# Vision mamba block with attention: scores over 64 rows, step sizes over 128 rows, and a scratch computation ahead of the loop

## The chip, the core and the metric

The kernel runs on one core of a Trainium2 chip. The metric is the device time of one execution in microseconds (us). The kernel before took 6128.99 us, the median of three runs (6116.84, 6128.99 and 6130.85). All data are float32.

## The reference, cut to what matters

For each of 32 images (the first 16 are "large", the others "small") the reference builds 274 tokens of 192 channels, passes them through a bidirectional selective scan, and then through a block with attention and an MLP:

```python
# per image: x is (274, 192)
h = concat([cls, patches @ W + b]) + pos_emb, then concat text      # 1 + 196 + 77 = 274 tokens
# mixer, for the forward and the backward direction
dt_lo, B, C = split(conv_silu(xi) @ x_proj)                         # dt_lo has 12 values per token
dt = softplus(dt_lo @ dt_w + dt_b)                                  # 384 step sizes per token
state = exp(dt * A) * state + (dt * u) * B;  y = state . C          # 16 states per channel
# attention, 12 heads of 16 values
a = softmax((q @ k.T) * 16 ** -0.5);  o = a @ v;  x = x + o @ w_proj + b_proj
# small images: the gated sum of three variants of the attention and of the MLP
x = x + gelu(ln(x) @ w1 + b1) @ w2 + b2
```

## The kernel before, in words

One step of the program handles one image (b) and interleaves three stages that belong to different images: the scans of image b in both directions, the fine part (layer norms, attention, MLP) of the image before it (f, ending with e), and the front part (patch projection, input projection, convolution, step sizes) of the image after it (a). A step is cut into 2 x 18 "gaps". Each engine has its own instruction stream, written out by hand: in every gap it issues its share of the scan, then its share of the fine part, then its share of the front. Two loops (7 iterations for large and 6 for small images, two steps in each) hold 26 of the 32 steps, the other six are written out; before them stands `front()`, after them `finish()`, in which only the last fine part is left and nothing overlaps it. Order is kept by semaphores alone: each engine works its list strictly in order and stops at a wait.

- VectorE (DVE) carries the scan (`scan_step`): in a cycle of three gaps it multiplies (L936, 128x2192), scans (L953) and multiplies again (L957). L936 may start only when TensorE has summed the states of two half-units before (`ysum`, L417). DVE also takes the row maxima of the scores (L1062), the reciprocal of the row sums (L1069) and the products with it (L1072).
- ScalarE (ACT) computes the decays (L715), the exponentials of the softmax (L788) and most copies out of PSUM; `qk_copy` (L773) copies queries and keys of a group of four heads from PSUM to `qk`, scaling the queries by -1/4.
- TensorE (PE) sums the 8 state rows with an identity matrix (L417) and does all projections. `scores` (L530) multiplies, for each of 12 heads and 3 tiles of 92 queries, 16 rows of queries by 16 rows of keys: head hd of a group lies in the rows 32 * (hd % 4) to 32 * (hd % 4) + 16, and the 16 rows behind it are zero, since the projection weights are spaced with zeros. `turn` (L542) transposes the probabilities, `av` (L551) multiplies them by the values. `dt_mm` (L479) computes the step sizes over 13 rows: 12 of `dt_lo` and one of ones for the bias. Every float32 matmul appears in the trace as two matmul records.
- Each of `qk_mms`, `qk_copy` and `scores` is done per group: group 0 in gaps 11 to 13, group 1 in gaps 17 to 18, group 2 in gaps 22 to 23. In PE's list the scores of a head wait for the copies of the group, and from the second head on for the exponentials of the head before.
- In `front()`, SyncE (SP) loads the patches, the text and 14 weights; DVE fills constants, waits for all weights (semaphore s_w), derives some constants from them and raises s_c to 20; PE and ACT wait for that before the first image. GpSimd (POOL) only makes the identity matrix and a mask.

## Time and profile before

| | |
|---|---|
| median of three runs | 6128.99 us (6116.84 to 6130.85) |
| span of the profiled execution | 6123.8 us; the page gives no time of that execution beside its span; the median is 5.2 us above the span |
| busy: DVE, PE, ACT, POOL | 5554.8, 5309.5, 3780.6, 0.8 us |
| mean granted TensorE clock | 0.874 of full speed |
| weights landed, first instruction that needed them | 25.72 us |

The span is the time from the first to the last instruction. Busy shares are means over the whole span. In rows of the trace, "PEclk" is the granted clock of TensorE: 1.00 is 2.4 GHz, 0.50 is 1.2 GHz, and values between are a mix of the two over the stretch. "idle before <-releaser" is how long the engine had done nothing, and what ended that.

### The profile page before, as it was taken

Reading aid. Unit: us, or ns where it says so; the run is one execution under the profiler, and the core shown is the slowest. Engines: PE = TensorE matmul, PEld = TensorE weight load, DVE = VectorE, ACT = ScalarE, POOL = GpSimd, SP = SyncE. Lnnn points to the kernel's source line nnn. Section 1 sums busy time; section 2 is a strip of 40 time slices with the busy share of each in tenths; the row PEclk is TensorE's granted clock in tenths of the full one; section 3 lists DMA queues with packets and bytes.
Section 4 is the critical chain, followed back from the end, with each engine's and each line's share of the span. In section 5 each row is a group of like instructions: output and inputs, shape, how many; then the busy total and the mean of one; then the engine's idle time right before and its main releaser. Section 6 shows DMA issues by size and latency. Waiting matters only on the chain.

```text
span 6123.8 us, 74116 instructions
## 1 busy us (share of the span) xinstructions
PE 5309.5 (87%) x22816; PEld 3509.9 (57%) x22816; DVE 5554.8 (91%) x6069; ACT 3780.6 (62%) x9506; POOL 0.8 (0%) x8
## 2 busy tenths in 40 slices
PE   5788888888888888888889999888998989989888
PEld 3555555555555555555556655655656556556554
DVE  6999999999999999999999999998999989999962
ACT  3566666656666556666666666666666666666643
POOL 0000000000000000000000000000000000000000
PEclk7898888888888888888989988898888888889885
DMA  3211211211211211211221111111111212112100
GB/s 101 64 45 57 64 45 53 66 51 51 64 52 46 66 58 44 65 53 44 65 65 42 60 60 38 64 58 44 64 45 54 66 37 65 50 47 65 40 23 2
DMA packets 56934, 327.85 MB, mean 54 GB/s; under 512 B 13246, under 2 KB 15742, under 8 KB 23627
## 3 DMA queue, kind: packets, MB, share of 16 engines
q1 hardware_dynamic: 56490, 322.53, 16.6%
q8 instruction: 207, 3.39, 0.2%
q14 instruction: 237, 1.93, 0.1%
HBM read 313.52 MB, written 8.98 MB: 53 GB/s over the span
## 4 chain that ended last, share of the span: by engine, by line
PE 40%; DVE 33%; issue 20%; ACT 6%; DVEq 1%; DMA 0%; SPq 0%; ACTq 0%
DVE hs L953 12%; PE y_ps L417 10%; PE f_ps L530 7%; DVE hs L936 4%; PE f_ps L542 4%; DVE hs L957 4%; PE f_ps L581 3%; PE f_ps L496 2%; PE a_ps L455 2%; DVE neg_max L1062 2%; DVE xc L1016 2%; PE f_ps L511 2%; PE f_ps L592 2%; PE f_ps L487 2%; PE a_ps L465 1%
## 5 line engine op out<-in xcount | busy, mean ns | idle before, releaser
L953 DVE TENSOR_TENSOR_SCAN hs<-decay,hs 128x2192 f32<-128x2192 f32 x384 | 1811.1, 4717 | 28.0 <-issue 19.7
L417 PE MATMUL y_ps<-hs,ident 128*128 128x274 f32 x5376 | 1719.8, 455 | 89.5 <-issue 31.3
L715 ACT ACTIVATE decay<-dt,inner_s 128x273 f32<-128x273 f32 x3072 | 1380.6, 513 | 75.7 <-issue 40.3
L417 PEld LDWEIGHTS y_ps<-hs,ident 128*128 128x128 f32 x5376 | 1104.1, 217 | 480.8 <-issue 187.8
L936 DVE TENSOR_TENSOR hs<-b_rows,dtu 128x2192 f32<-128x2192 f32 x384 | 935.5, 2436 | 99.2 <-PE y_ps L417 76.7
L957 DVE TENSOR_TENSOR hs<-hs,c_rows 128x2192 f32<-128x2192 f32 x384 | 934.7, 2434 | 3.4
L530 PE MATMUL f_ps<-qk 16*92 16x274 f32 x2304 | 733.5, 458 | 227.9 <-ACT hid L788 216.4
L805 ACT ACTIVATE hid<-f_ps 92x273 f32<-92x273 f32 (+1 forms) x1152 | 421.7, 393 | 556.6 <-PE f_ps L542 552.4
L788 ACT ACTIVATE hid<-f_ps,neg_max 92x274 f32<-92x274 f32 x1152 | 544.0, 480 | 301.1 <-DVE neg_max L1062 300.9
L530 PEld LDWEIGHTS f_ps<-qk 16*92 16x92 f32 x2304 | 350.7, 174 | 549.2 <-ACT hid L788 344.6
L542 PE MATMUL f_ps<-ident,hid 92*92 92x92 f32 x3456 | 514.7, 286 | 86.8 <-ACT hid L805 48.7
L542 PEld LDWEIGHTS f_ps<-ident,hid 92*92 92x92 f32 x3456 | 386.0, 148 | 341.6 <-issue 162.1
L1062 DVE TENSOR_REDUCE neg_max<-f_ps 92x1 f32<-92x274 f32 x1152 | 446.8, 430 | 72.0 <-PE f_ps L530 69.4
L455 PE MATMUL a_ps<-xn,w_in_s 96*128 96x274 f32 x1536 | 464.7, 428 | 8.5 <-ACT xi L738 4.9
L496 PE MATMUL f_ps<-res,centre_w 96*96 96x274 f32 x768 | 238.0, 460 | 202.6 <-DVE res L1040 128.6
L722 ACT ACTIVATE hid<-f_ps 96x548 f32<-96x548 f32 x128 | 79.2, 619 | 465.5 <-PE f_ps L496 465.5
L455 PEld LDWEIGHTS a_ps<-xn,w_in_s 96*128 96x128 f32 x1536 | 304.8, 209 | 90.9 <-issue 15.5
L592 PE MATMUL f_ps<-hid,fc_s 128*96 128x274 f32 x1152 | 294.5, 409 | 53.2 <-ACT hid L826 51.3
L1016 DVE SCALAR_TENSOR_TENSOR xc<-xi,inner_s,xc 128x274 f32<-128x274 f32 x576 | 289.6, 504 | 20.1
L496 PEld LDWEIGHTS f_ps<-res,centre_w 96*96 96x96 f32 x768 | 134.4, 186 | 296.0 <-DVE res L1040 142.4
L592 PEld LDWEIGHTS f_ps<-hid,fc_s 128*96 128x96 f32 x1152 | 192.7, 169 | 145.7 <-ACT hid L826 63.7
L819 ACT ACTIVATE hid<-f_ps,fc_b_s 128x274 f32<-128x274 f32 x384 | 183.1, 490 | 136.7 <-PE f_ps L581 136.7
(103 smaller groups left out, 5773.8 us busy)
## 6 DMA issues: line engine op xcount, KB each, us to landing
b_rows<-bc_rows SPq DMA_DIRECT2D x128, 1096.0 KB, 5.6
c_rows<-bc_rows SPq DMA_DIRECT2D x128, 1096.0 KB, 5.6
xp<-in_patches SPq DMA_DIRECT2D x32, 588.0 KB, 7.4
out<-h SPq DMA_DIRECT2D x32, 205.5 KB, 2.2
bc_rows<-bc_s SPq DMA_DIRECT2D x64, 34.2 KB, 1.5
h<-in_txt SPq DMA_DIRECT2D x32, 57.8 KB, 2.3
w_in_s<-in_w_in SPq DMA_DIRECT2D x1, 1152.0 KB
fc_s<-in_fc SPq DMA_DIRECT2D x2, 576.0 KB
```

The lines of the kernel that those rows point to most:

```text
L417: mm = pe.matmul(y_ps[:, 0:T], ident[:, :], hs[q % 2][:, n, :], start=(q % 2 == 0 and n == 0), stop=(q % 2 == 1 and n == end - 1))
L455: mm = pe.matmul(a_ps[:, j % 2, 0:T], w_in_s[:, i, d, j * 128:(j + 1) * 128], xn[parity(b)][:, i, :], start=(i == 0), stop=(i == 1))
L496: mm = pe.matmul(f_ps[0:CH, o, 0:T], centre_w[:, int(i != o), :], x[:, i, :], start=(i == 0), stop=(i == 1))
L530: pe.matmul(f_ps[0:QT, t, 0:T], qk[r:r + HD, 0, QS[t]:QS[t] + QT], qk[r:r + HD, 1, :], start=True, stop=True).then_inc(sc_mm, 1)
L542: mm = pe.transpose(f_ps[0:QT, 3 + n % 2, k * QT:(k + 1) * QT], prob[hd % 2][:, t, QS[k]:QS[k] + QT], ident[0:QT, 0:QT])
L592: mm = pe.matmul(f_ps[0:CH, VARIANTS[v][2][i], 0:T], fc2_s[:, ch, i * CH:(i + 1) * CH], hid[:, HC * v + ch, :], start=(ch == 0), stop=(ch ...
L715: e = act.activation(decay[half][:, n, t], dt[d][:, u, t], ACT.Exp, scale=inner_s[:, d, u, s:s + 1])
L788: act.activation(prob[hd % 2][:, t, :], f_ps[0:QT, t, 0:T], ACT.Exp, scale=-1.0, bias=neg_max[:, hd % 2, t:t + 1], accum_out=row_sum[:, hd ...
L936: dve.tensor_tensor(x[:, :, :], states[half][:, :, :], dtu[d][:, u, :].unsqueeze(1).broadcast_to([128, NH, T]), ALU.mult).then_inc(dbu_don ...
L953: dve.tensor_tensor_scan(i, a, i, 0.0, ALU.mult, ALU.add).then_inc(scan_done, 1)
L957: dve.tensor_tensor(x[:, :, :], x[:, :, :], reads[half][:, :, :], ALU.mult)\
L1062: dve.tensor_reduce(neg_max[:, hd % 2, t:t + 1], f_ps[0:QT, t, 0:T], AX_X, ALU.min)\
```

## The change

Three things, in one diff.

1. Scores contract over 64 rows. ACT now makes two copies of the queries of a group, each multiplied by a column of `q_scale` that is -1/4 in the rows of the even (or the odd) heads and 0 elsewhere, and one of the keys: three copies in place of two. A score matmul takes 64 rows (two heads); the rows of the other head are zero in the masked copy.
2. Step sizes contract over 128 rows. `dt_w_s` and `dt_lo` are widened to 128 rows; POOL zeroes all of `dt_w_s` before SP loads its 13 rows, and SP waits for that before the first weight.
3. A scratch computation in the prologue, whose results nothing uses: 17 counted instructions on DVE, 9 products on POOL, 20 matmuls on PE over 32 or 64 rows (40 records in a trace), and 2 exponentials on ACT. DVE reaches the wait for the weights only when all four are done. ACT's table load moves ahead of it.

```diff
--- before.py
+++ after.py
@@ -126,7 +126,7 @@
         w_in_s = sb("w_in_s", [CH, 2, 2, 2 * INNER])
         inner_s = sb("inner_s", [128, 2, IC, INNER_W])
         x_proj_s = sb("x_proj_s", [128, 2, IC, 32 + 2 * N])
-        dt_w_s = sb("dt_w_s", [RANK + 1, 2, INNER])
+        dt_w_s = sb("dt_w_s", [128, 2, INNER])
         w_out_s = sb("w_out_s", [128, 2, IC, C])
         w_qk_s = sb("w_qk_s", [CH, 2, 2, GROUPS * 128])
         w_v_s = sb("w_v_s", [CH, 2, C + HD])
@@ -141,6 +141,7 @@
         mean_w = sb("mean_w", [CH, CH])
         centre_w = sb("centre_w", [CH, 2, CH])
         v_mask = sb("v_mask", [QT, 3])
+        q_scale = sb("q_scale", [128, 2])
         eps_c = sb("eps_c", [128, 1])
         one_c = sb("one_c", [128, 1])
 
@@ -159,13 +160,13 @@
         dt = [sb(f"dt{d}", [128, IC, T]) for d in range(2)]
         dtu = [sb(f"dtu{d}", [128, IC, T]) for d in range(2)]
         bc_s = sb("bc_s", [32 + 2 * N, T])
-        dt_lo = sb("dt_lo", [RANK + 1, T])
+        dt_lo = sb("dt_lo", [128, T])
         states = [sb(f"b_rows{i}", [128, NH, T]) for i in range(2)]
         reads = [sb(f"c_rows{i}", [128, NH, T]) for i in range(2)]
         decay = [sb(f"decay{i}", [128, NH, T]) for i in range(2)]
         hs = [sb(f"hs{i}", [128, NH, T]) for i in range(2)]
         yg = sb("yg", [128, UNITS, T])
-        qk = sb("qk", [128, 2, T])
+        qk = sb("qk", [128, 3, T])
         v_s = sb("v_s", [QT, 3, C + HD])
 
         hid = sb("hid", [128, 3 * HC, T])
@@ -190,6 +191,10 @@
         s_cp = sem("constants_pool")
         s_ca = sem("constants_act")
         s_x = sem("patches_loaded")
+        p_dve = sem("probe_vector")
+        p_pool = sem("probe_pool")
+        p_pe = sem("probe_tensor")
+        p_act = sem("probe_scalar")
         s_txt = [sem(f"txt_loaded{i}") for i in range(2)]
 
         tok_mm = sem("tok_mm")
@@ -267,7 +272,7 @@
         out_stored = sem("out_stored")
 
         LOADS = [(tok_w_s, tok_w), (feat_s, feat), (w_in_s, w_in), (inner_s, inner), (x_proj_s, x_proj),
-                 (dt_w_s, dt_w), (w_out_s, w_out), (w_qk_s, w_qk), (w_v_s, w_v), (w_proj_s, w_proj),
+                 (dt_w_s[0:RANK + 1, :, :], dt_w), (w_out_s, w_out), (w_qk_s, w_qk), (w_v_s, w_v), (w_proj_s, w_proj),
                  (fc1_s, fc1), (fc1_b_s, fc1_b), (fc2_s, fc2), (gate, gumbel)]
         CONSTS = 20
 
@@ -364,6 +369,7 @@
             def front():
                 load_patches((0, 0))
                 load_txt((0, 0))
+                sp.wait_ge(s_cp, 1)
                 for dst, src in LOADS:
                     sp.dma_start(dst[tuple(slice(None) for _ in dst.shape)], src).then_inc(s_w, 16)
                 spread_rows((0, 0), 0)
@@ -389,13 +395,23 @@
 
         @block.gpsimd
         def _(pool):
+            pool.memset(dt_w_s[:, :, :], 0.0).then_inc(s_cp, 1)
             pool.memset(ident[:, :], 0.0).then_inc(s_cp, 1)
             pool.memset(v_mask[:, :], 1.0).then_inc(s_cp, 1)
-            pool.wait_ge(s_cp, 2)
+            pool.wait_ge(s_cp, 3)
             pool.affine_select(out=ident[:, :], in_=ident[:, :], compare_op=ALU.not_equal, fill=1.0, base=0,
                                pattern=[[-1, 128]], channel_multiplier=1).then_inc(s_cp, 1)
 
             pool.memset(v_mask[0:1, 1:3], 0.0).then_inc(s_cp, 1)
+            pool.memset(q_scale[:, :], 0.0).then_inc(s_cp, 1)
+            pool.wait_ge(s_cp, 6)
+            for r in range(4):
+                pool.memset(q_scale[32 * r:32 * r + 32, r % 2:r % 2 + 1], -HD ** -0.5).then_inc(s_cp, 1)
+            pool.wait_ge(s_cp, 10)
+            pool.wait_ge(p_dve, 7)
+            for n in range(9):
+                wait(pool, p_pool, n)
+                pool.tensor_tensor(hs[1][:, 4:8, :], hid[:, 0:4, :], hid[:, 4:8, :], ALU.mult).then_inc(p_pool, 1)
 
 
         @block.tensor
@@ -520,14 +536,14 @@
                     mm.then_inc(v_mm, 1)
 
             def scores(f, hd):
-                g, r = hd // 4, 32 * (hd % 4)
-                pe.wait_ge(qk_copied, at(f, 2 * GROUPS, 2 * g + 2))
+                g, rows = hd // 4, slice(64 * (hd % 4 // 2), 64 * (hd % 4 // 2) + 64)
+                pe.wait_ge(qk_copied, at(f, 3 * GROUPS, 3 * g + 3))
                 if hd == 0:
                     pe.wait_ge(v_copied, at(f, 3, 3))
                 for t in range(3):
                     if hd > 0:
                         pe.wait_ge(pexp, at(f, 3 * HEADS, 3 * hd - 2 + t))
-                    pe.matmul(f_ps[0:QT, t, 0:T], qk[r:r + HD, 0, QS[t]:QS[t] + QT], qk[r:r + HD, 1, :],
+                    pe.matmul(f_ps[0:QT, t, 0:T], qk[rows, hd % 2, QS[t]:QS[t] + QT], qk[rows, 2, :],
                               start=True, stop=True).then_inc(sc_mm, 1)
 
             def turn(f, hd, lo, hi):
@@ -674,9 +690,27 @@
                             out_proj(b, (UNITS - 2,))
                         fronts(b, d, a, gap)
 
+            def scratch():
+                pe.wait_ge(s_cp, 10)
+                pe.wait_ge(p_dve, 17)
+                for _ in range(2):
+                    for r in range(4):
+                        rows = slice(32 * r, 32 * r + 32)
+                        mm = pe.matmul(f_ps[0:QT, r, 0:T], ident[rows, 0:QT], hid[rows, 0, :], start=True, stop=True)
+                for _ in range(3):
+                    for r in range(2):
+                        rows = slice(32 * r, 32 * r + 32)
+                        mm = pe.matmul(f_ps[0:QT, r, 0:T], ident[rows, 0:QT], hid[rows, 0, :], start=True, stop=True)
+                for _ in range(3):
+                    for r in range(2):
+                        rows = slice(64 * r, 64 * r + 64)
+                        mm = pe.matmul(f_ps[0:QT, r, 0:T], ident[rows, 0:QT], hid[rows, 0, :], start=True, stop=True)
+                mm.then_inc(p_pe, 1)
+
             def front():
+                scratch()
                 pe.wait_ge(s_w, 16 * len(LOADS))
-                pe.wait_ge(s_cp, 4)
+                pe.wait_ge(s_cp, 10)
                 pe.wait_ge(s_c, CONSTS)
                 b = (0, 0)
                 tok(b, (0, 1))
@@ -765,13 +799,13 @@
                 act.activation(v, v, ACT.Ln, bias=one_c[:, 0:1]).then_inc(sp_ln, 1)
 
             def qk_copy(f, g):
-                for s in range(2):
-                    act.wait_ge(qk_mm, at(f, 2 * GROUPS, 2 * g + s + 1))
-                    if s == 0:
-                        wait(act, sc_mm, at(f, 3 * HEADS, 12 * g))
-
-                    act.activation(qk[:, s, :], f_ps[:, s, 0:T], ACT.Copy, scale=(-HD ** -0.5, 1.0)[s])\
+                act.wait_ge(qk_mm, at(f, 2 * GROUPS, 2 * g + 1))
+                wait(act, sc_mm, at(f, 3 * HEADS, 12 * g))
+                for odd in range(2):
+                    act.activation(qk[:, odd, :], f_ps[:, 0, 0:T], ACT.Copy, scale=q_scale[:, odd:odd + 1])\
                         .then_inc(qk_copied, 1)
+                act.wait_ge(qk_mm, at(f, 2 * GROUPS, 2 * g + 2))
+                act.activation(qk[:, 2, :], f_ps[:, 1, 0:T], ACT.Copy).then_inc(qk_copied, 1)
 
             def v_copy(f):
                 for t in range(3):
@@ -893,10 +927,13 @@
                             fine_late(*part)
 
             def front():
+                act.preload_act_table_set("natural_log_exp_and_others")
+                act.wait_ge(p_pe, 1)
+                act.activation(hid[0:QT, 9:11, :], f_ps[0:QT, 0:2, 0:T], ACT.Exp, scale=-1.0).then_inc(p_act, 1)
+                act.activation(hid[0:QT, 11:13, :], f_ps[0:QT, 0:2, 0:T], ACT.Exp, scale=-1.0).then_inc(p_act, 1)
                 act.wait_ge(s_w, 16 * len(LOADS))
-                act.wait_ge(s_cp, 4)
+                act.wait_ge(s_cp, 10)
                 act.wait_ge(s_c, CONSTS)
-                act.preload_act_table_set("natural_log_exp_and_others")
                 act.activation(inner_s[:, :, :, I_A:I_A + N], inner_s[:, :, :, I_A:I_A + N], ACT.Exp).then_inc(s_ca, 1)
                 b = (0, 0)
                 squares(xn[0][:, :, :], sq_a, a_cen, 1, a_sq)
@@ -1178,6 +1215,52 @@
                             fine(*part)
                         fronts(b, d, a, gap)
 
+            def scratch():
+                u = f_ps[:, 0:3, :].rearrange("p b t -> p (b t)")
+                u_in = u[:, 0:4 * T]
+                u_row = u[:, 4 * T:5 * T]
+                a = hid[:, 0:4, :].rearrange("p n t -> p (n t)")
+                o = hs[1][:, 0:4, :].rearrange("p n t -> p (n t)")
+                dec = decay[1][:, 0:4, :].rearrange("p n t -> p (n t)")
+                dve.memset(hid[:, :, :], 0.5).then_inc(p_dve, 1)
+                dve.memset(decay[1][:, :, :], 0.5).then_inc(p_dve, 1)
+                dve.wait_ge(p_dve, 2)
+                dve.tensor_tensor(u_in, a, dec, ALU.mult).then_inc(p_dve, 1)
+                dve.wait_ge(p_dve, 3)
+                dve.tensor_tensor_scan(o, dec, u_in, 0.0, ALU.mult, ALU.add).then_inc(p_dve, 1)
+                dve.wait_ge(p_dve, 4)
+                dve.tensor_scalar(u_row, hid[:, 0, :], 0.5, None, ALU.mult).then_inc(p_dve, 1)
+                dve.wait_ge(p_dve, 5)
+                dve.tensor_tensor(u_in.rearrange("p (n t) -> p n t", n=4), hid[:, 0:4, :],
+                                  u_row.unsqueeze(1).broadcast_to([128, 4, T]), ALU.mult).then_inc(p_dve, 1)
+                dve.wait_ge(p_dve, 6)
+                dve.tensor_tensor_scan(o, dec, u_in, 0.0, ALU.mult, ALU.add).then_inc(p_dve, 1)
+                dve.wait_ge(p_pool, 1)
+                dve.wait_ge(p_dve, 7)
+                dve.tensor_tensor_scan(o, dec, u_in, 0.0, ALU.mult, ALU.add).then_inc(p_dve, 1)
+                dve.wait_ge(p_dve, 8)
+                dve.tensor_tensor(u_in.rearrange("p (n t) -> p n t", n=4), hid[:, 0:4, :],
+                                  u_row.unsqueeze(1).broadcast_to([128, 4, T]), ALU.mult).then_inc(p_dve, 1)
+                dve.wait_ge(p_dve, 9)
+                dve.tensor_tensor_scan(o, dec, u_in, 0.0, ALU.mult, ALU.add).then_inc(p_dve, 1)
+                dve.wait_ge(p_dve, 10)
+                dve.scalar_tensor_tensor(out=decay[1][:, 4, :], in0=u_row, scalar=0.5, in1=hid[:, 9, :],
+                                         op0=ALU.mult, op1=ALU.add).then_inc(p_dve, 1)
+                dve.tensor_reduce(neg_max[:, 0, 0:2], f_ps[0:QT, 0:2, 0:T], AX_X, ALU.min).then_inc(p_dve, 1)
+                dve.wait_ge(p_dve, 12)
+                dve.tensor_scalar(u_row, hid[:, 0, :], 0.5, None, ALU.mult).then_inc(p_dve, 1)
+                dve.wait_ge(p_dve, 13)
+                dve.tensor_tensor(u_row, hid[:, 0, :], hid[:, 1, :], ALU.mult).then_inc(p_dve, 1)
+                dve.wait_ge(p_dve, 14)
+                dve.tensor_tensor(decay[1][:, 5, :], hid[:, 0, :], hid[:, 1, :], ALU.mult).then_inc(p_dve, 1)
+                dve.wait_ge(p_dve, 15)
+                dve.tensor_tensor(u_in, a, dec, ALU.mult).then_inc(p_dve, 1)
+                dve.wait_ge(p_dve, 16)
+                dve.tensor_tensor_scan(o, dec, u_in, 0.0, ALU.mult, ALU.add).then_inc(p_dve, 1)
+                dve.wait_ge(p_pool, 9)
+                dve.wait_ge(p_dve, 17)
+                dve.wait_ge(p_act, 2)
+
             def front():
 
                 dve.memset(mean_w[:, :], 1.0 / C).then_inc(s_c, 1)
@@ -1185,6 +1268,7 @@
                 dve.memset(one_c[:, :], 1.0).then_inc(s_c, 1)
                 dve.memset(xi[:, :, :], 0.0).then_inc(s_c, 1)
                 dve.memset(dt_lo[:, :], 1.0).then_inc(s_c, 1)
+                scratch()
                 dve.wait_ge(s_w, 16 * len(LOADS))
                 for i in range(2):
 
@@ -1199,7 +1283,7 @@
                 dve.tensor_reduce(gate_sum[:, 0:1], gate[:, 0:3], AX_X, ALU.add).then_inc(s_c, 1)
                 dve.tensor_copy(gate_sum[:, 1:2], gate[:, 0:1]).then_inc(s_c, 1)
                 dve.wait_ge(s_c, 14)
-                dve.wait_ge(s_cp, 4)
+                dve.wait_ge(s_cp, 10)
                 dve.tensor_tensor(centre_w[:, 0, :], ident[0:CH, 0:CH], mean_w[:, :], ALU.subtract).then_inc(s_c, 1)
                 dve.tensor_scalar(centre_w[:, 1, :], mean_w[:, :], -1.0, None, ALU.mult).then_inc(s_c, 1)
                 for i in range(2):
```

## Rows read from the trace of the kernel before

**Rows 1.** The page: busy us (share) and instructions of each engine.

```profile
PE 5309.5 (87%) x22816; PEld 3509.9 (57%) x22816; DVE 5554.8 (91%) x6069; ACT 3780.6 (62%) x9506; POOL 0.8 (0%) x8
```

**Rows 2.** DVE's waits, whole span: us in total, times, longest us.

```profile
DVE hs L936 <- PE y_ps L417: 76.7, 77, 1.9
DVE neg_max L1062 <- PE f_ps L530: 69.4, 76, 8.0
DVE row_inv L1069 <- ACT hid L788: 27.3, 19, 2.5
```

**Rows 3.** DVE's waits in the last attention, 5985 to 6075 us; same columns.

```profile
DVE neg_max L1062 <- PE f_ps L530: 47.8, 29, 8.0
DVE row_inv L1069 <- ACT hid L788: 7.5, 3, 2.5
```

**Rows 4.** Windows: length, busy us (count) of PE, PEld, DVE, ACT, POOL, PEclk, DMA.

```profile
2085.00:2090.00 5.00, 5.00 (x24) 3.75 (x23) 4.26 (x4) 3.50 (x8) 0.00 (x0) 1.00 0.00 0
2105.00:2110.00 5.00, 5.00 (x16) 3.25 (x15) 4.96 (x9) 1.68 (x5) 0.00 (x0) 0.50 0.71 226
2097.00:2174.00 77.00, 68.75 (x318) 43.55 (x319) 75.48 (x112) 55.77 (x169) 0.00 (x0) 0.83 0.14 45
2174.00:2277.00 103.00, 88.11 (x376) 61.25 (x374) 96.58 (x76) 57.61 (x123) 0.00 (x0) 0.95 0.20 64
5985.00:6070.00 85.00, 72.69 (x283) 40.51 (x282) 24.57 (x72) 39.58 (x129) 0.00 (x0) 0.56 0.00 1
```

**Rows 5.** Timeline: start, us, engine, line, count; two waits, and scores at 0.50.

```profile
2088.45 2.44 DVE L936 TENSOR_TENSOR hs<-b_rows,dtu 128x2192 f32<-128x2192 f32 x1 [0.74 <-PE y_ps L417]
2361.89 2.44 DVE L936 TENSOR_TENSOR hs<-b_rows,dtu 128x2192 f32<-128x2192 f32 x1 [1.91 <-PE y_ps L417]
6040.23 3.01 PE L530 MATMUL f_ps<-qk 16*92 16x274 f32 x6 [1.04 <-ACT hid L788]
```

**Rows 6.** Timeline around the copies of group 1, step at 2071 us.

```profile
2119.94 2.43 DVE L936 TENSOR_TENSOR hs<-b_rows,dtu 128x2192 f32<-128x2192 f32 x1
2120.50 0.92 ACT L773 ACTIVATE qk<-f_ps 128x274 f32<-128x274 f32 x2
2121.55 1.61 PE L530 MATMUL f_ps<-qk 16*92 16x274 f32 x6 [0.33 <-ACT qk L773]
2122.73 0.90 DVE L1062 TENSOR_REDUCE neg_max<-f_ps 92x1 f32<-92x274 f32 x2
```

**Rows 7.** Timeline around the copies of group 2, same step.

```profile
2146.11 1.62 PE L530 MATMUL f_ps<-qk 16*92 16x274 f32 x6
2149.87 1.13 DVE L1062 TENSOR_REDUCE neg_max<-f_ps 92x1 f32<-92x274 f32 x3
```

**Rows 8.** Groups by line and shape: busy us, mean ns | idle before.

```profile
L953 DVE TENSOR_TENSOR_SCAN hs<-decay,hs 128x2192 f32<-128x2192 f32 x384 | 1811.1, 4717 | 28.0 <-issue 19.7 <-DVE decay L943 1.5
L961 DVE TENSOR_TENSOR hs<-hs 128x1096 f32<-128x1096 f32 x96 | 124.8, 1300 | 3.3
L773 ACT ACTIVATE qk<-f_ps 128x274 f32<-128x274 f32 x192 | 76.7, 400 | 90.7 <-PE f_ps L511 84.1
L417 PE MATMUL y_ps<-hs,ident 128*128 128x274 f32 x5376 | 1719.8, 455 | 89.5 <-issue 31.3 <-DVE hs L961 29.8 <-DVE yg L970 20.9
L479 PE MATMUL a_ps<-dt_lo,dt_w_s 13*128 13x274 f32 x384 | 140.8, 447 | 6.6 <-DVE dt L1022 5.9 <-ACT dt_lo L750 0.5
```

**Rows 9.** Timeline of the prologue.

```profile
1.12 0.76 DVE L1186 MEMSET xi<- 128x840 f32 x1
1.22 0.29 POOL L395 TENSOR_SCALAR_AFFINE_SELECT ident<-ident 128x128 f32<-128x128 f32 x1 [0.23 <-POOL v_mask L393]
1.97 0.58 SPq L368 DMA_DIRECT2D tok_w_s<-in_tok_w  x1
25.72 0.23 DVE L1192 TENSOR_TENSOR h<-feat_s 96x1 f32<-96x1 f32 x2 [23.56 <-DMA gate<-in_gumbel]
27.86 5.88 PE L429 MATMUL a_ps<-xp,tok_w_s 128*96 128x196 f32 x24 [27.86 <-DVE bias_sum L1207]
```

## Prediction

> **What bounds the kernel now.** I read the page's busy times first, then DVE's waits, the clock in windows, and the timeline. DVE is busy 5554.8 of 6123.8 us [rows 1], so 569 us of the span are time in which DVE idles, and the change touches no DVE instruction of the loop: the loop can only gain from that idle time. Much of it lies outside the loop's steps (in the prologue and in the last image's fine part, which nothing overlaps), or waits for things that the change doesn't touch, such as the layer norms' rstd. Three waits can hang on the scores' stretch. The row maxima wait for score matmuls: 69.4 us, of which 47.8 are in the last attention, so 21.6 in the steps [rows 2, 3]. The reciprocal waits for the exponentials: 27.3 less 7.5, 19.8 us. L936 waits for the state sums: 76.7 us in 77 waits, but most of these come once or twice per image at full clock as a fixed 0.74 us (one is shown; I count about 48 of 0.74 to 0.77), some 36 us; the rest, about 41 us, sits 14 to 20 us behind the last scores of an image and reaches 1.91 us each [rows 2, 5]. Together 82 us.
>
> That these waits are tied to the clock is what the windows show. From 2174 to 2277 us, mostly outside the attention, the granted clock is 0.95; from 2097 to 2174, the attention of the same image, it is 0.83 [rows 4]. In the attention PE is no idler: from 2105 to 2110 it is busy all 5 us and yet granted 0.50, while from 2085 to 2090 it is as busy at 1.00. What differs is what it does: before 2105 it does scores over 16 rows and transposes, before 2085 state sums over 128 rows. In the last attention (5985 to 6070) it is busy 72.69 of 85 us at 0.56 [rows 4]. I read this as a clock that falls where matmuls use few rows, though busy. The change makes the same matmuls use 64.
>
> **The change part by part.**
>
> *Score matmuls.* 2304 records stay 2304; six take 1.61 us at 1.00 and 3.01 at 0.50 [rows 5, 6]. More rows need no more time at a given clock: the 13-row step sizes take 447 ns on average, about the 455 ns of the 128-row state sums [rows 8]. I take 0 directly. The gain is the clock. Upper bound: all 82 us. Lower bound: nothing. The attention's dips to 0.50 come in two kinds: where PE is busy with few rows, and where it idles, waiting for DVE or ACT. Four times the rows in the scores should remove the first kind and leave the second. I take half, 41 us, and expect the clock of such an attention to go from 0.83 to about 0.90, and the mean of the span from 0.874 to about 0.90.
>
> *Last attention.* DVE, ACT and PE follow one another here, so time at 0.50 counts in full: 12 heads x (3.01 - 1.61) = 16.8 us for the scores alone. But PE idles between heads and the transposes keep their rows, so I expect the clock to stay mostly low and take a quarter, 4 us (0 to 17).
>
> *Step sizes over 128 rows.* 384 records, same columns: 0. They lie outside the low stretches, so no clock is bought either. The wider `dt_lo` memset has the same 274 columns.
>
> *Third copy.* 96 more copies of 0.40 us [rows 8], 38 us on ACT, which is 62% busy. The scores of a group wait for all copies, so for group 1 the first score starts 0.40 us later. Timeline: DVE's L936 ends at 2119.94 + 2.43 = 2122.37, the scores run from 2121.55 to 2123.16, and the maxima end at 2122.73 + 0.90 = 2123.63, right behind the scores; 0.40 us later the last maximum ends about 0.3 us later [rows 6]. 31 x 0.3 = 9 us. For group 2 scores begin at 2146.11 and the maxima only at 2149.87, since DVE is in its product [rows 7]: hidden, and if that cover went it would be 12 us. Group 0 lies a gap and more ahead of its scores. Behind the copy in ACT's list stand three decays of the next scan, with slack. In the last attention 3 x 0.40 = 1 us. Sum 10 us, between 0 and 38.
>
> *SP's wait for the zeroed weights.* SP's first weight goes out at 1.97; POOL starts a memset of 768 columns at about 0.75 and needs 1 to 2 us by its 0.29 us for 128 columns [rows 9]. At most 0.6 us, on loads that no longer set the end, below.
>
> *Scratch.* Before, DVE passes the wait for the weights at 25.72 [rows 9]. Now it gets there when the scratch is done. DVE starts it at about 2.2. Memsets of 4932 and 2192 columns at 0.76 us for 840: 6.4. Four products of 1096 columns at 1.30: 5.2. Five scans of 1096 columns at half of 4.717: 11.8. Six small ones, the maximum over 548 columns counted twice, 7 x 0.45: 3.1 [rows 6, 8, 9]. Before the third scan DVE waits for POOL's first product. No row has one; DVE's 1.30 is the floor, POOL's select (0.29 for 128 columns, so 2.5 for 1096) the nearest row and the ceiling; I take 2.5. DVE is done at 31.2. POOL's nine products start at 16.4 and end at 38.9, under what follows. Then PE's 40 records: 0.27 each at full clock is 10.8 us; at 0.50 all the way 20; and 4.3 if matmuls of different row groups overlap (16 in place of 40). I take 10.8, end 42.0. Then two exponentials over 548 columns, 0.8 each by the copies: 43.6. The wait for weights is long over, so the prologue is longer by 43.6 - 25.7 = 17.9. One credit: PE's first 24 projection records, 5.88 us now, would take 24 x 0.27 x 196/274 = 4.6 if the scratch has raised the clock. Net +17 us, between 9 (POOL at 1.3, PE at 4.3) and 27 (PE at 20, no credit). The earlier table load gives nothing: it stood beside PE's first projections.
>
> The Trainium skill (TensorE: Matmul & The Clock Gate, Part 3: Packing small matmuls) says that matmuls in distinct row groups run concurrently; no row here shows it. By it the scratch would take PE 4.3 us and the total would be 6 us lower.
>
> *Sum.* -41 - 4 + 10 + 17 = -18. The page gives the span, 6123.8, and not the time of its execution; the span lies 5.2 us under the median, within the spread of the three runs, and the differences apply to both: 6129 - 18 = 6111 us, a span of 6106.
>
> **The rivals.**
>
> *The clock doesn't care about rows (slower).* If the dips come from something else that scores and transposes share (their short bursts, the waits between heads), 64 rows buy nothing and only the costs stay: 6129 + 10 + 17 = 6156, 6138 to 6194 with their bounds. For it speaks that the dips also come where PE waits; against it, the 5 us at 0.50 with PE busy all through [rows 4]. It decides from the point where the clock gives back less than 27 us. The Trainium skill's page TensorE: Matmul & The Clock Gate (Part 1, What's actually happening) says that the gate follows how busy PE has been, with no word of rows; its Part 4 says that transposes don't count as busy in the same way. By that rule the scores already count in full and this rival is what happens, at 6156; the busy 5 us at 0.50 speak against its first half, and partly for its second.
>
> *The clock rises, DVE does not profit.* The attention's clock goes up, but PE's work arrives in time anyway: DVE is busy 75.48 of 77 us there [rows 4]. Waits for state sums stay, as the dip behind the last scores comes from PE idling. Then the gain is some 10 us: 6129 - 10 + 27 = 6146. For it: 1.5 us of idle time in a whole attention. Against: the 1.91 and the reciprocal's waits.
>
> *The clock stays up through every attention.* All 82 us and the tail's 17 go: 6129 - 82 - 17 + 27 = 6057. Against: dips where PE has nothing to do, which no row count cures.
>
> **How the numbers follow.** My forecast has a chance of 0.45, with its own range 6090 to 6132; the clock without regard to rows 0.17; no profit 0.22; full clock 0.16. A measurement here tells 0.3% from no change, 18 us: below 6110.6 is faster, above 6147.4 slower. The forecast stands on that bound and gives 0.27 to faster and 0.18 to same; the full clock 0.16 to faster; no profit 0.19 to same and 0.03 to slower; the first rival 0.06 to same and 0.11 to slower. Faster 0.43, same 0.43, slower 0.14. The range takes in most of the outer cases: 6070 to 6155. I name 6111.
>
> **What would show it.** In the profile after: mean clock near 0.90, and above 0.87 in an attention of the middle of the run (else the first rival). The reciprocal's waits and the row maxima's outside the last attention should halve (else no profit). The six score records of a head still take 1.61 us at full clock. Copies x288 at 0.40. The first projection at about 45 rather than 27.9; its start is the price of the scratch, and if it is near 35 matmuls overlapped. The prediction fails if the low stretches merely move to the projections behind the attention, or if ACT's third copy holds up scores of every group.

## The result, and the profile after

The changed kernel took 6066.69 us (median of four runs, 6062.72 to 6075.44), 0.990 of the time of before (0.988 to 0.992). I had predicted 6111 and a range of 6070 to 6155: the direction was right and the size was not.

The page of the changed kernel: span, then busy us (share) and instructions of each engine.

```profile
span 6065.1 us, 74390 instructions
PE 5150.6 (85%) x22856; PEld 3475.0 (57%) x22856; DVE 5575.6 (92%) x6086; ACT 3813.9 (63%) x9604; POOL 25.4 (0%) x23
```

DVE is busy 20.8 us longer than in [rows 1], the scratch, and yet the span is 58.7 us shorter. So DVE idled about 80 us less. Where it stopped idling, DVE's waits over the whole span of the changed kernel (us in total, times, longest us):

```profile
DVE neg_max L1099 <- PE f_ps L546: 50.1, 32, 8.2
DVE hs L973 <- PE y_ps L433: 38.6, 64, 1.2
DVE row_inv L1106 <- ACT hid L822: 10.9, 9, 2.5
```

They answer to [rows 2], with the lines moved by the edit: L936 is L973, L1062 is L1099, L1069 is L1106. The wait for state sums is half of what it was, and its longest fell from 1.9 to 1.2 us. Of the row maxima's 50.1 us, 49.7 are in the last attention (5920 to 6016 us), where [rows 3] had 47.8: in the steps that wait is gone, and in the last attention it has not shrunk.

Windows of the changed kernel, to set beside [rows 4]: the attention of a large image, the stretch behind it, the attention of a small image, and the last attention (length, busy us (count) of PE, PEld, DVE, ACT, POOL, PEclk, DMA share, GB/s).

```profile
2106.00:2183.00 77.00, 67.81 (x319) 42.19 (x320) 75.98 (x111) 57.60 (x172) 0.00 (x0) 0.83 0.14 44
2183.00:2286.00 103.00, 85.48 (x378) 61.67 (x376) 96.72 (x81) 58.79 (x128) 0.00 (x0) 0.96 0.21 64
4104.00:4181.00 77.00, 66.00 (x320) 41.50 (x321) 75.96 (x112) 57.18 (x172) 0.00 (x0) 0.87 0.14 45
5928.00:6008.00 80.00, 69.29 (x267) 38.33 (x265) 24.58 (x72) 39.39 (x128) 0.00 (x0) 0.53 0.00 1
```

The same window over a small image in the kernel before:

```profile
4112.00:4189.00 77.00, 69.88 (x313) 44.61 (x314) 74.22 (x111) 54.42 (x164) 0.00 (x0) 0.78 0.14 45
```

The small image's clock rose from 0.78 to 0.87. The large image's window shows 0.83 again: a mean over one hand-cut window depends on where it is cut and on the image. So I took the same stretch in every image, from the start of its first score to the start of its last one. The mean granted clock there is 0.863 before and 0.894 after for large images, 0.813 and 0.899 for small ones, and 0.558 and 0.534 in the last attention, whose stretch takes 68.0 and 69.6 us. Behind the scores, up to the first score of the next image, it stayed where it was (0.898 and 0.894 for large images, 0.929 and 0.928 for small ones), so the low stretches did not move there. The mean clock of the whole span is 0.894 (0.874 before).

### The profile page after: what moved, and what is told of

Its sections match the earlier page's. It is cut to its first block, busy times and chain, and to the rows that moved or that the text cites. A ratio compares the mean times of both kernels' runs of the same rounds, so it can differ in the third digit from the quotient of the medians.

```text
span 6065.1 us, 74390 instructions
## 1 busy us (share of the span) xinstructions
PE 5150.6 (85%) x22856; PEld 3475.0 (57%) x22856; DVE 5575.6 (92%) x6086; ACT 3813.9 (63%) x9604; POOL 25.4 (0%) x23
## 4 chain that ended last, share of the span: by engine, by line
DVE 41%; PE 28%; issue 23%; ACT 6%; DVEq 1%; ACTq 0%; DMA 0%; POOL 0%; POOLq 0%
DVE hs L990 14%; PE y_ps L433 6%; DVE hs L973 5%; DVE hs L994 4%; DVE neg_max L1099 4%; PE f_ps L546 4%; PE f_ps L597 3%; DVE xc L1053 3%; PE f_ps L608 3%; PE f_ps L512 3%; PE f_ps L503 2%; PE f_ps L558 2%; DVE hid L1109 2%; ACT hid L822 2%; PE a_ps L471 1%
## 5 line engine op out<-in xcount | busy, mean ns | idle before, releaser
L433 PE MATMUL y_ps<-hs,ident 128*128 128x274 f32 x5376 | 1643.9, 440 | 80.2 <-DVE hs L998 29.8
L433 PEld LDWEIGHTS y_ps<-hs,ident 128*128 128x128 f32 x5376 | 1091.8, 212 | 407.7 <-issue 113.7
L973 DVE TENSOR_TENSOR hs<-b_rows,dtu 128x2192 f32<-128x2192 f32 x384 | 935.3, 2436 | 63.1 <-PE y_ps L433 38.6
L546 PE MATMUL f_ps<-qk 64*92 64x274 f32 x2304 | 712.0, 448 | 294.2 <-ACT hid L822 275.7
L546 PEld LDWEIGHTS f_ps<-qk 64*92 64x92 f32 x2304 | 339.7, 172 | 609.9 <-ACT hid L822 414.4
L558 PE MATMUL f_ps<-ident,hid 92*92 92x92 f32 x3456 | 479.5, 272 | 106.5 <-DVE hid L1109 68.7
L558 PEld LDWEIGHTS f_ps<-ident,hid 92*92 92x92 f32 x3456 | 357.1, 139 | 343.6 <-issue 143.0
L1099 DVE TENSOR_REDUCE neg_max<-f_ps 92x1 f32<-92x274 f32 x1152 | 437.7, 428 | 51.8 <-PE f_ps L546 50.1
## 6 DMA issues: line engine op xcount, KB each, us to landing
bc_rows<-bc_s SPq DMA_DIRECT2D x64, 34.2 KB, 1.5
```

Source lines behind the costliest of these rows:

```text
L433: mm = pe.matmul(y_ps[:, 0:T], ident[:, :], hs[q % 2][:, n, :], start=(q % 2 == 0 and n == 0), stop=(q % 2 == 1 and n == end - 1))
L546: pe.matmul(f_ps[0:QT, t, 0:T], qk[rows, hd % 2, QS[t]:QS[t] + QT], qk[rows, 2, :], start=True, stop=True).then_inc(sc_mm, 1)
L558: mm = pe.transpose(f_ps[0:QT, 3 + n % 2, k * QT:(k + 1) * QT], prob[hd % 2][:, t, QS[k]:QS[k] + QT], ident[0:QT, 0:QT])
L973: dve.tensor_tensor(x[:, :, :], states[half][:, :, :], dtu[d][:, u, :].unsqueeze(1).broadcast_to([128, NH, T]), ALU.mult).then_inc(dbu_don ...
L1099: dve.tensor_reduce(neg_max[:, hd % 2, t:t + 1], f_ps[0:QT, t, 0:T], AX_X, ALU.min)\
```

## The experiments

All kernels in one table. Ratios are to the kernel before, with the 95% interval. The columns prologue, loop and tail split the profiled span into the prologue (up to the first patch addition), the loop, and the tail (from the last image's patch addition). "Three waits" are DVE's for state sums, row maxima and reciprocals, between the prologue and the last fine part.

| kernel | median us | ratio (interval) | mean clock | prologue | loop | tail | three waits |
|---|---|---|---|---|---|---|---|
| before | 6129.9 | 1 | .874 | 33.9 | 5566.8 | 523.2 | 118.0 |
| after | 6066.7 | .990 (.988, .992) | .894 | 57.0 | 5495.4 | 512.7 | 42.4 |
| e1 no scratch | 6058.4 | .989 (.987, .991) | .895 | 34.7 | 5509.1 | 512.8 | 38.9 |
| e2 scores alone | 6071.4 | .991 (.990, .993) | .899 | 34.4 | 5524.6 | 518.5 | 82.3 |
| e3 copies, 16 rows | 6146.8 | 1.004 (1.002, 1.005) | .872 | 33.3 | 5580.3 | 530.3 | 127.3 |
| e4 scratch alone | 6121.9 | 1.000 (.999, 1.001) | .877 | 57.1 | 5529.9 | 530.8 | |
| e5 e1 + 20 fills | 6048.7 | .986 (.984, .988) | .892 | 34.6 | 5499.1 | 512.6 | |
| e6 32 rows, 2 copies | 6074.5 | .990 (.988, .992) | .887 | 33.4 | 5520.0 | 516.6 | 81.7 |
| e7 128 rows, 5 copies | 6047.4 | .986 (.984, .988) | .929 | 34.8 | 5517.6 | 489.2 | 78.7 |
| e8 step sizes alone | 6134.3 | 1.000 (.999, 1.001) | .866 | 35.2 | 5588.3 | 525.6 | 95.4 |
| e9 before + 20 fills | 6115.2 | .997 (.996, .999) | .871 | 34.2 | 5569.9 | 527.5 | |
| e10 no POOL products | 6060.9 | .988 (.986, .990) | .892 | 47.8 | 5499.5 | 512.7 | |
| e11 e2 + 20 fills | 6060.1 | .989 (.986, .991) | .902 | 34.5 | 5505.9 | 516.0 | |
| e12 best version | 6030.6 | .983 (.982, .985) | .896 | 33.6 | 5503.1 | 492.1 | |

The median of before is the one measured beside the changed kernel; beside e1 to e4 it was 6126.3, beside e5 to e8 6131.6, beside the others 6131.0. A profile is of one execution: those of e2, e8 and e9 were 8, 17 and 18 us longer than their kernels' medians, so their splits are read with care.

The experiments keep small parts of the changed kernel's prologue: all but e9 zero `dt_w_s` on POOL ahead of the weights' loads, fill `q_scale`, and load ACT's table early, also where the steps don't need it. Without the scratch their prologues lie within 1.3 us of before's 33.9, so "alone" below is meant for the steps.

### Rows or copies: e1, e2, e3, e6, e7

**e1** is the change without its third part.

```diff
-                scratch()          # PE and DVE
-            for n in range(9):     # POOL's products
-                act.activation(hid[0:QT, 9:11, :], ...)   # and the second exponential
```

> The change without the scratch computation (scores over 64 rows, three copies, step sizes over 128 rows). If the scratch costs only what it adds ahead of the first projection (23.2 us from the first tile's addition in the two traces, 33.85 against 57.02), this takes 23 us less than the changed kernel: about 6044 us, ratio 0.986 to before, with the clock of the changed kernel, 0.89. Rival: the scratch shifts the loop against the clock's own rhythm or leaves the clock high, and part of the gain in the loop is its doing; then this is no faster than the changed kernel, 6060 or more.

It came 8 us under the changed kernel, but the intervals overlap: the whole gain is there without the scratch. Of the two expectations the second came true: no 23 us are saved with it.

**e2** also takes the step sizes back to 13 rows.

```diff
-        dt_w_s = sb("dt_w_s", [128, ...])
-        dt_lo = sb("dt_lo", [128, T])
+        dt_w_s = sb("dt_w_s", [RANK + 1, ...])
+        dt_lo = sb("dt_lo", [RANK + 1, T])
```

> Only the scores are changed (64 rows, three copies); the step sizes stay at 13 rows, no scratch. If the step sizes do nothing, this equals the kernel without the scratch within 0.2%, about 6044 us. Rival: the 128 rows of the step sizes hold the clock up in the gaps before the next scores (or at the loop's turn), and without them 10 to 30 us come back.

**e3** keeps e2's three copies, the masks included, and lets the scores contract over 16 rows as before. It differs from e2 in nothing but the rows that each score matmul reads.

```diff
-                g, rows = hd // 4, slice(64 * (hd % 4 // 2), 64 * (hd % 4 // 2) + 64)
+                g, rows = hd // 4, slice(32 * (hd % 4), 32 * (hd % 4) + HD)
```

> The same three copies and masked queries, but each score matmul takes 16 rows again; all else as in the kernel with the scores alone changed. Work, waits and order are the same; only the rows differ. If the rows raise the clock, the mean clock falls back to 0.87 and the time goes to before plus the third copy: 6130 to 6140 us. Rival: the gain comes from the third copy's delay shifting the steps, not from rows; then this keeps the gain and takes 6044 to 6060.

This is the pair that decides: 6146.8 against 6071.4 us, with intervals far apart. The same instructions, the same columns, and 64 rows in place of 16 are worth 75 us. It took a little more than the 6130 to 6140 I had expected of it. DVE's waits outside the prologue and the last fine part show how. Those of e3:

```profile
DVE hs L947 <- PE y_ps L428: 76.2, 76, 1.9
DVE row_inv L1080 <- ACT hid L799: 25.7, 22, 1.3
DVE neg_max L1073 <- PE f_ps L541: 25.4, 51, 3.8
DVE yg L981 <- PE y_ps L428: 23.8, 13, 3.7
```

And those of e2, same columns:

```profile
DVE hs L947 <- PE y_ps L428: 66.3, 76, 1.9
DVE yg L981 <- PE y_ps L428: 17.6, 7, 3.6
DVE row_inv L1080 <- ACT hid L799: 9.4, 9, 1.3
DVE neg_max L1073 <- PE f_ps L541: 6.6, 16, 0.5
```

The waits for state sums, row maxima and reciprocals fall from 127.3 to 82.3 us, 45 of the 55.7 us by which the loop is shorter, and `yg` gives 6 more. The score matmuls themselves don't change at a given clock (shortest and median record 389 ns over 16 rows, 391 over 64); it is the granted clock of the stretch that rises, from .850 to .895 for large images and from .814 to .888 for small ones. The state sums profit most: 5376 records average 456 ns in e3 and 440 in e2. Two other readings fall away. PE is not busier in e2, but less so (5180.5 of 6077.5 us against 5324.5 of 6144.0). And the weight loader's unexplained idle time ahead of the state sums, which matters in e8's part below, is the same in both (190.9 and 188.6 us).

**e6** asks whether the rows must hold data. Its steps are those of the kernel before, with scores that read the 16 rows of zeros behind each head as well, and no third copy.

```diff
-                    pe.matmul(f_ps[0:QT, t, 0:T], qk[r:r + HD, 0, QS[t]:QS[t] + QT], qk[r:r + HD, 1, :],
+                    pe.matmul(f_ps[0:QT, t, 0:T], qk[r:r + 2 * HD, 0, QS[t]:QS[t] + QT], qk[r:r + 2 * HD, 1, :],
```

> The kernel before with score matmuls over 32 rows in place of 16: the 16 rows behind each head are zero already, so no masked copy is needed and there are two copies as before. If the clock follows the rows, it lies between 0.874 and 0.90 and the time between: 6095 to 6120 us. If it needs rows with values other than zero, nothing happens: 6129.

Rows of zeros on both sides raise the clock too, and this one line in the steps, at 6074.5, already equals e2 and beats my range of 6095 to 6120: 32 rows give less clock (.868 and .851 in the score stretches of large and small images) and save the third copy.

**e7** goes the other way: 128 rows, one masked copy of the queries per head, five copies per group. (`dt_lo` lies in the rows of `bc_s` here; nothing else differs from e2.)

```diff
-                for odd in range(2):
-                    act.activation(qk[:, odd, :], f_ps[:, 0, 0:T], ACT.Copy, scale=q_scale[:, odd:odd + 1])\
+                for odd in range(4):
+                    act.activation(qk[:, odd, :], f_ps[:, 0, 0:T], ACT.Copy, scale=q_scale[:, odd:odd + 1])\
...
-                    pe.matmul(f_ps[0:QT, t, 0:T], qk[rows, hd % 2, QS[t]:QS[t] + QT], qk[rows, 2, :],
+                    pe.matmul(f_ps[0:QT, t, 0:T], qk[:, hd % 4, QS[t]:QS[t] + QT], qk[:, 4, :],
```

> Score matmuls over all 128 rows, with four masked copies of the queries and one of the keys per group (five copies, against three), step sizes at 13 rows, no scratch. If rows raise the clock further: clock 0.93 or more in the middle attentions and the last one at full clock too; but the two further copies cost about 20 us each by the third one's price. Gain 40 to 80, cost 40: 6030 to 6100 us. Rival: the clock is at its ceiling with 64 rows and only the copies count: 6110.

The clock follows again: .952 and .943 in the stretches, and for the first time also in the last attention. Windows of e7 over a small image's attention and over the last one (columns as above):

```profile
3920.00:3997.00 77.00, 61.87 (x320) 41.58 (x321) 75.67 (x112) 59.05 (x176) 0.00 (x0) 0.91 0.15 45
5928.00:5975.00 47.00, 35.54 (x216) 22.21 (x215) 22.29 (x65) 34.04 (x115) 0.00 (x0) 0.96 0.00 1
```

That stretch takes 47.6 us in place of 68.0, and the tail falls from e2's 518.5 to 489.2. In the loop 128 rows give only 7 us over 64, since two more copies stand against them and DVE has little left to win at these waits: 16, 32, 64 and 128 rows put the three at 127 (or 118 with two copies), 82, 82 and 79 us. That the copies hold the rest back is argued, not isolated.

### Step sizes over 128 rows: e8 beside e1 and e2

**e8** is the kernel before with that part alone.

```diff
-        dt_lo = sb("dt_lo", [RANK + 1, T])
+        dt_lo = sb("dt_lo", [128, T])
```

> The kernel before with the step sizes over 128 rows alone (no scratch, scores over 16 rows). From the two kernels with 64-row scores (6058 with, 6071 without) it should gain 13 us: 6113. Rival: that difference was the phase of the loop, and this one is within 5 us of before.

Alone it changes nothing (0.9999, 0.9986 to 1.0012). I had expected 6113. Beside the 64-row scores it is worth 13 us (e2 to e1), and 11 with the fills of the next part (e11 to e5). Both pairs have intervals that touch, so the size is uncertain; but the cause can be read. Timeline of e2 (start, us, engine, line, count, idle before):

```profile
3903.29 2.12 PE L522 MATMUL f_ps<-cen,w_qk_s 96*128 96x274 f32 x8 [0.43 <-DVE cen L1001]
...
3905.34 0.29 PEld L490 LDWEIGHTS a_ps<-dt_lo,dt_w_s 13*128 13x128 f32 x2 [0.36 <-issue]
3905.34 0.72 PE L490 MATMUL a_ps<-dt_lo,dt_w_s 13*128 13x274 f32 x2
...
3905.99 0.76 PEld L428 LDWEIGHTS y_ps<-hs,ident 128*128 128x128 f32 x4 [0.36 <-issue]
3906.00 1.19 PE L428 MATMUL y_ps<-hs,ident 128*128 128x274 f32 x4
...
3907.32 2.44 DVE L947 TENSOR_TENSOR hs<-b_rows,dtu 128x2192 f32<-128x2192 f32 x1 [0.74 <-PE y_ps L428]
```

And of e1 at the same place of the step:

```profile
3894.94 2.12 PE L522 MATMUL f_ps<-cen,w_qk_s 96*128 96x274 f32 x8 [0.82 <-DVE cen L1001]
...
3896.67 0.42 PEld L490 LDWEIGHTS a_ps<-dt_lo,dt_w_s 128*128 128x128 f32 x2
3896.90 0.63 PE L490 MATMUL a_ps<-dt_lo,dt_w_s 128*128 128x274 f32 x2
...
3897.13 0.88 PEld L428 LDWEIGHTS y_ps<-hs,ident 128*128 128x128 f32 x4
3897.36 1.09 PE L428 MATMUL y_ps<-hs,ident 128*128 128x274 f32 x4
...
3898.58 2.44 DVE L947 TENSOR_TENSOR hs<-b_rows,dtu 128x2192 f32<-128x2192 f32 x1 [0.35 <-PE y_ps L428]
```

The clock is 1.00 in both. With 128 rows each weight load starts 0.23 us ahead of its matmul, beside the one before. With 13 rows it starts with its matmul, after an idle 0.36 us of the loader, and so does the load of the state sums behind it. From the start of L522 to DVE's next product it is 4.03 us in e2 and 3.64 in e1; DVE waits 0.74 in place of 0.35, the same 0.39 more. This is the wait that I had read as fixed. The median record of a step-size matmul is 493 ns in e2 and 394 in e1, with nearly the same shortest (389 and 392): the mean of 447 that I had put beside the 455 ns of the state sums hid it. These waits are most of the ones that I had counted as 48: between 0.7 and 0.8 us there are 48 before, 56 in e2 and 11 in e1, and e1 has 34 between 0.30 and 0.37 us, where e2 has none. The Trainium skill (TensorE: Matmul & The Clock Gate, Part 3: Packing small matmuls) has weight loads overlap running matmuls only where the row groups differ; here loads of 128 rows did run beside matmuls over the same rows, and the load of 13 rows did not. The measurement decides, and it bears the page out only in part.

Why e8 alone gains nothing: its wait for state sums fell too, from 76.7 to 38.3 us outside the last fine part, while the waits for row maxima and `yg` rose from 21.5 and 15.9 to 40.1 and 45.1. What DVE gains at one wait it loses at the next as long as PE itself is late in the attention. And the clock fell: the median of the mean clocks is .867 in e8's twelve runs and .872 in those of the kernel before beside them, and the score stretches of large images have .836 in place of .863 (those of small ones .824 against .813). With the step sizes widened the clock also fell in the two other pairs, from .902 to .894 (e2 to e1) and from .902 to .892 (e11 to e5). So "more rows, more clock" holds for the scores and not for every matmul. Why it falls here no run isolates, and e8's profile is one of a longer execution.

### The scratch and where the loop's code lies: e4, e5, e9, e10, e11

**e4** has the steps of the kernel before, with the scratch (the third part of the change).

> The kernel before with the scratch computation alone. If it costs what it adds to the prologue, 6130 + 23 = 6153 us, ratio 1.004, clock 0.87. Rival: it changes the phase of the loop, or the clock at its start, and gives some of it back: 6100 to 6140.

It cost nothing (0.9998, 0.9987 to 1.0009), though its prologue is 23.2 us longer. The loop gave 37 us back and the tail took 8. DVE's waits told where 20 us of it came from; the rest stays open. Timeline of the kernel before at the start of a loop turn:

```profile
2027.39 2.44 DVE L936 TENSOR_TENSOR hs<-b_rows,dtu 128x2192 f32<-128x2192 f32 x1 [1.90 <-issue]
2033.34 4.73 DVE L953 TENSOR_TENSOR_SCAN hs<-decay,hs 128x2192 f32<-128x2192 f32 x1 [3.49 <-issue]
```

And its waits of this kind, in the steps:

```profile
DVE hs L936 <- issue: 21.7, 11, 2.2
DVE hs L953 <- issue: 19.7, 6, 3.5
```

Eleven turns start with some 2 us in which DVE waits for nothing that the profile shows. In the six turns of the large-image loop it stops once more, 3.3 us each, ahead of the first scan. The changed kernel has the first kind (22.9 us in 11) and not the second, and e4 likewise. The scratch does nothing there; it only moves the loop's instructions further on in DVE's stream, by 17 counted ones and their waits. So **e5** adds 20 trivial fills to e1, **e9** the same to the kernel before, **e11** to e2.

```diff
                 dve.memset(dt_lo[:, :], 1.0).then_inc(s_c, 1)
+                for n in range(20):
+                    dve.memset(hid[:, 17, n:n + 1], 1.0)
```

> The change without the scratch, with 20 fills of one column (0.06 us each) in VectorE's prologue, as many instructions as the scratch put into that list. Reason: the scan behind each turn of the first loop waits 2.5 to 3.7 us for nothing the trace shows, in every kernel without the scratch and in none with it (19.7 us in six waits before, 18.7 without the scratch, none after). If it is the place of the loop's code in VectorE's instruction stream that decides, the six waits go and this takes 6058 - 19 = 6039 us. Rival: the late start (the loop beginning 23 us later) or the work on the other engines does it; then the waits stay and it takes 6058.

> The kernel before with nothing but the 20 short fills in VectorE's prologue. If the place of the loop's code in VectorE's stream causes the six waits behind the turns of the first loop, they go (19.7 us) and this takes about 6110 us, ratio 0.997. Rival: the fills only shift the phase, or the waits need the scratch's late start; then 6130 with the six waits still there.

> Scores over 64 rows and the 20 fills, step sizes at 13 rows. The 128-row step sizes gave 13 us beside the 64-row scores (6058 against 6071) and nothing alone. If they do something of their own, this takes 6049 + 13 = 6062; if those 13 us came from the phase in which the loop settles, this is as likely as fast as the kernel with both, 6049.

In all three the scan's stop is gone, and the time falls by 10, 16 and 11 us (in the order e5, e9, e11), less than the stop itself in each. e9's interval excludes no change; the others' touch those of their partners. e5 came 10 us above what I had expected. All kernels without scratch or fills have it: 18.7, 19.4, 18.2, 19.6, 17.7 and 19.5 us in e1, e2, e3, e6, e7 and e8. That 20 fills ahead of the loop take the stop away, without the scratch and without a late start, is shown; that they do so by the place of the code is my reading of it, and which boundary it crosses is not shown.

**e10** is the changed kernel without POOL's nine products and DVE's waits for them.

```diff
-            for n in range(9):
-                wait(pool, p_pool, n)
-                pool.tensor_tensor(hs[1][:, 4:8, :], hid[:, 0:4, :], hid[:, 4:8, :], ALU.mult).then_inc(p_pool, 1)
```

> The changed kernel without GpSimd's nine products (VectorE, PE and ACT parts stay). In the changed kernel three VectorE products with two operands in SBUF took 2.69, 2.60 and 3.48 us beside GpSimd's products, against 0.45, 0.45 and 1.31 alone. If the two engines hold each other up, these three fall to that, and with GpSimd's first product (2.5 us) gone the prologue is 9 us shorter: 6058 us. Rival: the products are slow for another reason (two operands in SBUF of the same tile), and only 2.5 us go.

The prologue is 9.2 us shorter. The total falls by 6 us against the changed kernel, within the intervals. Three products of DVE in the changed kernel's timeline:

```profile
28.26 2.69 DVE L1253 TENSOR_TENSOR f_ps<-hid 128x274 f32<-128x274 f32 x1
30.98 2.60 DVE L1255 TENSOR_TENSOR decay<-hid 128x274 f32<-128x274 f32 x1
33.62 3.48 DVE L1257 TENSOR_TENSOR f_ps<-hid,decay 128x1096 f32<-128x1096 f32 x1
```

The same three in e10:

```profile
25.62 0.45 DVE L1248 TENSOR_TENSOR f_ps<-hid 128x274 f32<-128x274 f32 x1
26.10 0.45 DVE L1250 TENSOR_TENSOR decay<-hid 128x274 f32<-128x274 f32 x1
26.58 1.31 DVE L1252 TENSOR_TENSOR f_ps<-hid,decay 128x1096 f32<-128x1096 f32 x1
```

### The best version: e12

**e12** is e5, with the last image's scores alone over 128 rows: its masked copies go to a decay buffer that is free by then.

```diff
+                q, per = qk[:, hd % 2, :], 3
+                if last(f):
+                    rows, q, per = slice(0, 128), decay[0][:, hd % 4, :], 5
-                pe.wait_ge(qk_copied, at(f, 3 * GROUPS, 3 * g + 3))
+                pe.wait_ge(qk_copied, at(f, 3 * GROUPS, per * g + per))
...
-                for odd in range(2):
-                    act.activation(qk[:, odd, :], f_ps[:, 0, 0:T], ACT.Copy, scale=q_scale[:, odd:odd + 1])\
+                for odd in range(4 if last(f) else 2):
+                    dst, scale = (decay[0], head_scale) if last(f) else (qk, q_scale)
+                    act.activation(dst[:, odd, :], f_ps[:, 0, 0:T], ACT.Copy, scale=scale[:, odd:odd + 1])\
```

> A version meant to beat the changed kernel: no scratch, the 20 fills, 64-row scores in the steps, and in the last image, where nothing overlaps the attention, 128-row scores with four masked copies that lie in a free decay buffer. From the kernel with 128 rows everywhere, whose last part took 489 us against 513, this takes 6049 - 23 = 6026 us, with a clock near 0.96 in the last attention.

It took 6030.64 us (6024.19 to 6034.02), 0.983 of before (0.982 to 0.985), 36 us under the changed kernel. Window of e12 over the last attention, columns as above:

```profile
5912.00:5961.00 49.00, 37.69 (x218) 23.52 (x217) 22.46 (x65) 34.14 (x115) 0.00 (x0) 0.93 0.00 1
```

## Why the prediction was wrong, step by step

The chain from the kernel before over e3, e2 and e1 to the changed one has one part of the change in each link (the first also takes in the small parts of the prologue). By profiled spans (e2's lies 8 us high, which makes the second link look smaller and the third larger than by medians):

| link | prologue | loop | tail | sum | by medians | predicted |
|---|---|---|---|---|---|---|
| third copy (before to e3) | -0.6 | +13.5 | +7.1 | +20.0 | +20 | +10 |
| 64 rows (e3 to e2) | +1.1 | -55.7 | -11.8 | -66.4 | -75 | -45 |
| 128-row step sizes (e2 to e1) | +0.3 | -15.5 | -5.7 | -20.9 | -13 | 0 |
| scratch (e1 to after) | +22.3 | -13.7 | -0.1 | +8.5 | +8 | +17 |
| all | +23.1 | -71.4 | -10.5 | -58.8 | -60 | -18 |

**The step that failed most is "I take half, 41 us", with the 4 of the last attention.** The mechanism was right: busy matmuls over few rows pull the granted clock down, and the rows alone, with everything else kept, bring it back. The size was not, 75 us by the medians. The three waits I had named gave 45 us in the loop, close to the 41. But I had drawn the bound around these three, and the faster PE also shortened `yg`'s wait by 6 us, and the tail by 12. The attention before the last one lies in that tail (its clock is .72 in e3 and .90 in e2); I had counted only the last. In the last itself the step's "mostly low" held: .53. Its 4 us did not come: the stretch grew by 1.6 us. That is not the third copy, since e3 has three and takes the 68.0 us of before, while e9 with two copies and 16 rows takes 69.9 at .53: the stretch follows its clock, and between 16 and 64 rows nothing is to be had there.

**"Step sizes over 128 rows: 0" failed.** It was argued from mean durations. The row that spoke against it stood in the prediction: "most of these come as a fixed 0.74 us" at full clock, some 36 us, set aside as untouchable. Many of them fell to 0.35 with the 13-row matmul gone, around which the weight loads had stood still. From e2 to e1 the wait for state sums fell from 66.3 to 31.8 us; the waits of `yg`, of the MLP's addition and of the layer norms grew by 12, 8 and 5 us and took much of that back. 48 waits times 0.39 would have been 19 us; the loop gave 15.5, and by the medians the whole link gave 13.

**"Third copy +10" was half of what it cost.** I had the delay end at the row maxima of one group in an image. In e3 the row maxima wait 4 us longer than before (21.5 to 25.4), the reciprocals 6 (19.8 to 25.7) and `yg` 8 (15.9 to 23.8), and the loop is 13.5 us longer. The 7 us of the tail may not be the copy's at all: e4 and e9, with two copies, have tails of 530.8 and 527.5, like e3's 530.3. Copies by a column are also slower than I took them; groups of the changed kernel by line and shape (busy us, mean ns, idle before), to set beside L773 in [rows 8]:

```profile
L805 ACT ACTIVATE qk<-f_ps,q_scale 128x274 f32<-128x274 f32 x192 | 83.3, 490 | 65.8 <-PE f_ps L527 65.8
L808 ACT ACTIVATE qk<-f_ps 128x274 f32<-128x274 f32 x96 | 38.9, 405 | 4.5 <-PE f_ps L527 2.9
```

A group's copies keep ACT busy for (83.3 + 38.9) / 96 = 1.27 us in place of 0.80, so 0.47 more and not 0.40 (records overlap, so the means of 490 and 405 ns must not be added). The Trainium skill (ScalarE: Activation LUTs, What ACT_TABLE_LOAD costs) gives about 93 ns for each operand that is read per partition; the trace agrees, and I had not weighed it. In all ACT spends 45.5 us more on the copies.

**"Scratch +17" failed in two ways that partly cancel; it cost 8.** The prologue grew by 22.3 to 23.2 us, above 17.9 and with no credit worth having: the first projections still took 5.81 us (5.88 before). Its timeline in the changed kernel:

```profile
17.87 24.15 POOL L414 TENSOR_TENSOR hs<-hid 128x1096 f32<-128x1096 f32 x9 [15.01 <-DVE hs L1237]
39.72 2.15 PE L699 MATMUL f_ps<-hid,ident 32*92 32x274 f32 x16 [39.72 <-DVE hs L1259]
41.62 2.98 PE L703 MATMUL f_ps<-hid,ident 32*92 32x274 f32 x12
44.52 3.05 PE L707 MATMUL f_ps<-hid,ident 64*92 64x274 f32 x12
48.96 0.23 DVE L1276 TENSOR_TENSOR h<-feat_s 96x1 f32<-96x1 f32 x2 [9.39 <-ACT hid L933]
51.10 5.81 PE L445 MATMUL a_ps<-xp,tok_w_s 128*96 128x196 f32 x24 [3.53 <-DVE bias_sum L1291]
```

POOL's product took 2.68 us (I took 2.5). PE took 7.9 us, between my 10.8 and the 4.3 of full overlap. DVE was done at 39.6 and not at 31.2: 6.6 of these 8.4 us are the three products shown beside e10's. What I had not foreseen at all is the return: the loop became 13.7 us shorter, since the scan's 3.3 us in each of six turns went away.

**Right:** the mean clock (0.90 forecast, 0.894 measured) and that of an attention (about 0.90 forecast, .894 and .899 in the stretches, though the large image's window above shows 0.83, which by my own sign would have spoken for the first rival); that the waits of the reciprocal and of the row maxima in the steps would at least halve (19.8 to 3.4 and 21.5 to 0.4 us); that SP's wait and the wider fills cost about nothing (e1's prologue is 0.8 us longer than before's); the last attention's clock. **The first rival**, a clock that ignores rows, is refuted by e3 against e2. By the rule of the Trainium skill that I had set beside it (TensorE: Matmul & The Clock Gate, Part 1: What's actually happening), which speaks of how busy PE is and not of rows, e2 and e3 should have had one clock, or e3 the higher one, since its PE is the busier; they have .872 (e3) and .899 (e2). The second, that DVE does not profit, is refuted by the 45 us of waits. The third, full clock all through, did not happen either, though its 6057 is the nearest number: the attentions stand at .89 to .90 and the last one at .53. By the medians the rows gave 30 us more than I took, the step sizes 13 more and the scratch cost 9 less, against 10 more for the copy.

Open: why 128-row step sizes gain only beside the 64-row scores, and why the clock falls with them; what boundary the loop's code crosses, if that is it, and what shortened e4's loop by the other 17 us; and why DVE's turns start with 2 us of nothing.
